# Feed-forward stages: the gated layer of one sequence merged into the attention of the next, in one block without barriers

## The reference

```
residual = hidden_states
x = _rmsnorm(hidden_states, ln1_w)
attn = _attention(x, Wq, Wk, Wv, Wo)
mod = MOD_SCALE * jnp.tanh(attn @ A)
h = _rmsnorm(residual, ln2_w)
gate_pre = h @ W_in_base.T + mod * (h @ A) @ B
gate = jax.nn.silu(gate_pre)
up = h @ W_up_base.T
mlp_out = gate * up @ W_down.T
return residual + mlp_out
```

## Time and profile before

| | before |
|---|---|
| median of 3 runs | 6643.49 us (6639.04 to 6646.93) |
| span of the profiled execution | 6647.8 us |
| PE, share of the span | 86% |
| DVE, ACT, POOL | 48%, 43%, 34% |
| mean granted PE clock | 0.90 of full |

### The profile page before, as it was taken

The page is one execution under the profiler, slowest core; times in us unless marked ns, Lnnn a source line. Parts: engine busy times, 40 slices in busy tenths (PEclk is TensorE's granted clock), DMA queues, the critical chain, the costliest instruction groups (busy, mean ns, idle before and its releaser), DMA issues. The chain is left out here.

```text
span 6647.8 us, 126185 instructions
## 1 busy us (share of the span) xinstructions
PE 5714.2 (86%) x53008; PEld 3756.8 (57%) x53008; DVE 3169.6 (48%) x4553; ACT 2831.9 (43%) x5153; POOL 2288.6 (34%) x1583
## 2 busy tenths in 40 slices
PE   6888798865889868888888888888899988889999
PEld 5776566543666436666665666666444446664444
DVE  5555433334333247666666766666411135564111
ACT  2323333444344345555555555555411146663111
POOL 4444000001000037666666666666422210002222
PEclk8988788877887889999999999999899998889999
DMA  0000000000000000000000000000111100002111
GB/s 27 2 2 33 0 0 0 14 0 31 0 0 0 2 23 21 17 16 23 16 16 23 16 16 16 23 16 16 75 42 40 42 27 0 0 0 93 42 40 46
DMA packets 60565, 136.36 MB, mean 21 GB/s; under 512 B 11638, under 2 KB 24054, under 8 KB 58842
## 3 DMA queue, kind: packets, MB, share of 16 engines
q1 hardware_dynamic: 60122, 129.79, 5.8%
HBM read 127.26 MB, written 2.50 MB: 20 GB/s over the span
## 5 line engine op out<-in xcount | busy, mean ns | idle before, releaser
L599 PE MATMUL ps<-moe_xn_all,moe_w 128*128 128x512 f32 x1792 | 808.3, 594 | 1.6 <-DVE moe_h L712 1.6
L712 DVE TENSOR_TENSOR moe_h<-moe_silu,ps 128x512 f32<-128x512 f32 x224 | 153.9, 687 | 935.8 <-ACT moe_silu L654 928.7
L599 PEld LDWEIGHTS ps<-moe_xn_all,moe_w 128*128 128x128 f32 x1792 | 340.3, 191 | 424.4 <-issue 421.6
L1539 DVE SCALAR_TENSOR_TENSOR kda_cv<-kda_pre,kda_w_front,kda_cv 128x1024 f32<-128x1024 f32 x297 | 561.1, 1907 | 1.4
L654 ACT ACTIVATE moe_silu<-ps 128x512 f32<-128x512 f32 x224 | 133.7, 597 | 986.1 <-PE ps L599 986.0
L1716 POOL TENSOR_TENSOR kda_g<-kda_g,kda_f 128x512 f32<-128x512 f32 x225 | 421.6, 1874 | 279.6 <-DVE kda_rows L1708 270.4
L555 POOL TENSOR_TENSOR moe_h<-moe_h,moe_cb 128x512 f32<-128x512 f32 x176 | 233.6, 1327 | 696.5 <-DVE moe_h L712 696.5
L609 PE MATMUL ps<-moe_h,moe_w 128*128 128x512 f32 x896 | 420.4, 592 | 0.0
L1427 PE MATMUL ps<-kda_xn_all,kda_w_front 128*128 128x512 f32 x808 | 374.4, 607 | 24.9 <-DMA kda_w_front<-in_Kw 22.5
L1708 POOL TENSOR_TENSOR kda_rows<-kda_q,kda_f 128x512 f32<-128x512 f32 x225 | 357.2, 1588 | 88.3 <-POOL kda_f L1717 52.8
L1798 PE MATMUL ps<-kda_x_sb,kda_t 64*64 64x32 f32 x5120 | 310.1, 221 | 0.0
(11 more groups left out here) (506 smaller groups left out, 12804.7 us busy)
## 6 DMA issues: line engine op xcount, KB each, us to landing
kda_col<-kda_beta SPq DMA_DIRECT2D x34, 512.0 KB, 4.1
moe_w<-in_Mw SPq DMA_DIRECT2D x6, 2816.0 KB, 19.6
moe_cb<-kda_beta SPq DMA_DIRECT2D x64, 256.0 KB, 3.1
kda_w_front<-in_Kw SPq DMA_DIRECT2D x34, 455.0 KB, 4.8
moe_cb<-kda_beta SPq DMA_DIRECT2D x32, 224.0 KB, 2.9
kda_w_out<-in_Kw SPq DMA_DIRECT2D x32, 192.5 KB, 4.7
moe_cb<-kda_beta SPq DMA_DIRECT2D x32, 192.0 KB, 2.8
moe_cb<-kda_beta SPq DMA_DIRECT2D x32, 160.0 KB, 2.7
```

The source lines that it names most:

```text
L599: last = nc.tensor.matmul(ps_gu[u % 2][r], w13[:, k, i, r], n.xn[:, k, cols(c)], start=k == 0, stop=k == KD - 1)
L1539: ins = nc.vector.scalar_tensor_tensor(cv[i % 2][:], pre[i % 2][:, :, j:j + SEQ], w_vec(w, K_CONV + i * CONV + j), cv[i % 2][:], ALU.mult, ...
```

## The change

The second block of `ffn` is written anew. The hardware loop is gone: one block holds all 8 sequences, written out, with running semaphore counts and no barrier until the end of the stage. There are 9 rounds. Round b works the attention of sequence b, group by group, and between its parts the gated layer of sequence b-1, unit by unit: group s goes with unit s. Round 0 has attention alone, round 8 the gated layer alone. At the end of a round stand the projections of the following sequence, spread among the last steps of the attention.

To fit into PSUM, scores have one pair of banks (1, 2) in place of two, and gate and up of a unit share the halves of one bank (3); only in round 8 does a second bank (1) alternate with it. So `scores(i)` waits until group i-1 is masked, and `up(u)` until `h` of unit u-1 is done. On ACT, `copy_out` of a group now stands ahead of the exponentials of the next. SiLU is made from tanh: ACT takes tanh(x/2), and DVE makes (tanh + 1) * x and then 0.5 * that * up, two instructions in place of one. Exponential and tanh share a table, which is loaded once per stage in the first block. The copy `x_seq` (DVE L1098) is left out; the values are projected from `n.xn` itself.

```diff
...
+EXP_TANH = "exp_and_others"
...
-        x_seq = s.sb("x_seq", [P, KD, SEQ])
...
+        ps_s = psum(g, 1, GH * SEQ).rearrange("p (j k) -> p j k", j=GH)
...
-        ps_g = [psum(g, 1 + i, SEQ) for i in range(2)]
-        ps_u = [psum(g, 3 + i, SEQ) for i in range(2)]
-        ps_y = [psum(g, 5, SEQ), psum(g, 0, SEQ)]
...
+        def ps_gate(u):
+            return psum(g, 1 if u >= (BATCH - 1) * FFN_T and u % 2 else 3, SEQ)
+
+        def ps_up(u):
+            return psum(g, 1 if u >= (BATCH - 1) * FFN_T and u % 2 else 3, 2 * SEQ)[:, SEQ:]
...
+                nc.scalar.preload_act_table_set(EXP_TANH)
...
-        with nc.Fori(0, BATCH) as b:
-            with nc.Block() as block:
...
+                def scores(i):
+                    b, q, t = i // GROUPS, i % GROUPS // FQ, i % FQ
+                    pe.wait_ge(m.q_in_sb, b + 1)
+                    pe.wait_ge(m.k_in_sb, b + 1)
+                    if i > 0:
+                        pe.wait_ge(m.masked_ready, i)
+                    w = keys(i) * P
+                    for j in (0, 2, 1, 3):
+                        tile, row = head_at(t, j)
+                        rows = slice(32 * row, 32 * row + 32)
+                        last = nc.tensor.matmul(ps_s[:, j, 0:w], qt[rows, tile, q * P:(q + 1) * P],
+                                                kt[rows, tile, 0:w], start=True, stop=True)
+                    last.then_inc(m.scores_ready, 1)
...
+                def up(u):
+                    b, f = u // FFN_T, u % FFN_T
+                    if u >= 1:
+                        pe.wait_ge(m.h_ready, u - 1 if u > (BATCH - 1) * FFN_T else u)
+                    own = slice(f * P, (f + 1) * P)
+                    for k in range(KD):
+                        nc.tensor.matmul(ps_up(u), w_up[:, k, own], n.xn[:, k, cols(b)], start=k == 0,
+                                         stop=k == KD - 1)
+                    for k in range(KD):
+                        nc.tensor.matmul(ps_gate(u), w_in[:, k, own], n.xn[:, k, cols(b)], start=k == 0, stop=False)
+                    pe.wait_ge(m.mod_in_sb, b + 1)
+                    nc.tensor.matmul(ps_gate(u), low_b[:, own], mod[:], start=False, stop=True).then_inc(m.gu_ready, 1)
+
+                def down(u):
+                    f = u % FFN_T
+                    pe.wait_ge(m.h_ready, u + 1)
+                    for k in range(KD):
+                        last = nc.tensor.matmul(ps_y[k], w_down[:, f, k * P:(k + 1) * P], h[:, u % 2],
+                                                start=f == 0, stop=f == FFN_T - 1)
+                    last.then_inc(m.down_done, 1)
...
+                queries(0)
+                key_rows(0)
+                values(0)
+                for b in range(BATCH + 1):
+                    here, before = b < BATCH, b > 0
+                    for s_ in range(GROUPS):
+                        i, u = b * GROUPS + s_, (b - 1) * FFN_T + s_
+                        if here:
+                            scores(i)
+                        if before:
+                            up(u)
+                        if here and s_ >= 1:
+                            turn(i - 1)
+                        if before and s_ >= 1:
+                            down(u - 1)
+                        if here and s_ >= 2:
+                            pv(i - 2)
+                    if before:
+                        down(b * FFN_T - 1)
+                    if here:
+                        end = (b + 1) * GROUPS
+                        pv(end - 2)
+                        if b + 1 < BATCH:
+                            queries(b + 1)
+                        turn(end - 1)
+                        low(b)
+                        pv(end - 1)
+                        turn_shares(b)
+                        if b + 1 < BATCH:
+                            key_rows(b + 1)
+                        modulate(b)
+                        if b + 1 < BATCH:
+                            values(b + 1)
...
+                def half_gate(u):
+                    act.wait_ge(m.gu_ready, u + 1)
+                    if u >= 2:
+                        act.wait_ge(m.half_ready, u - 1)
+                    nc.scalar.activation(gate[:, u % 2], ps_gate(u), ACT.Tanh, scale=0.5).then_inc(m.gate_ready, 1)
+
+                query_copy(0)
+                key_copy(0)
+                for b in range(BATCH + 1):
+                    here, before = b < BATCH, b > 0
+                    for s_ in range(GROUPS):
+                        i, u = b * GROUPS + s_, (b - 1) * FFN_T + s_
+                        if before:
+                            half_gate(u)
+                        if here and s_ >= 1:
+                            copy_out(i - 1)
+                        if here:
+                            exps(i)
+                    if here:
+                        if b + 1 < BATCH:
+                            query_copy(b + 1)
+                        copy_out((b + 1) * GROUPS - 1)
+                        shares_copy(b)
+                        if b + 1 < BATCH:
+                            key_copy(b + 1)
+                        modulate(b)
...
+                def gated(u):
+                    dve.wait_ge(m.gate_ready, u + 1)
+                    if u >= 2:
+                        dve.wait_ge(m.down_done, u - 1)
+                    nc.vector.scalar_tensor_tensor(h[:, u % 2], gate[:, u % 2], 1.0, ps_gate(u), ALU.add,
+                                                   ALU.mult).then_inc(m.half_ready, 1)
+                    dve.wait_ge(m.half_ready, u + 1)
+                    nc.vector.scalar_tensor_tensor(h[:, u % 2], h[:, u % 2], 0.5, ps_up(u), ALU.mult,
+                                                   ALU.mult).then_inc(m.h_ready, 1)
...
+                values(0)
+                for b in range(BATCH + 1):
+                    here, before = b < BATCH, b > 0
+                    for s_ in range(GROUPS):
+                        if here:
+                            maxima(b * GROUPS + s_)
+                        if before:
+                            gated((b - 1) * FFN_T + s_)
+                    if before:
+                        residual(b - 1)
+                    if here:
+                        widen(b)
+                        outputs(b)
+                        modulate(b)
+                        if b + 1 < BATCH:
+                            values(b + 1)
+                dve.wait_ge(m.x_done, KD * BATCH)
+        s.barrier()
...
```

More of the change, by code:

```diff
@@ L967, in ffn @@
         gate, h = s.sb("gate", [P, 2, SEQ]), s.sb("h", [P, 2, SEQ])
[L968 to L974 removed]
+        qt, kt = s.sb("qt", [P, FQ, SEQ]), s.sb("kt", [P, FQ, SEQ])
@@ L1044, in _ @@
                     for t in range(QT):
+                        at = b * SEQ + t * P
                         for k in range(KD):
-                            last = nc.tensor.matmul(ps_v[:, t], x_seq[:, k, t * P:(t + 1) * P], wv[:, k],
-                                                    start=k == 0, stop=k == KD - 1)
-                    last.then_inc(t_.v_ready, 1)
-                    attn_pe(nc, g, t_, pe)
+                            last = nc.tensor.matmul(ps_v[:, t], n.xn[:, k, at:at + P], wv[:, k], start=k == 0,
+                                                    stop=k == KD - 1)
@@ new lines, in turn, with pv @@
+                def turn(i):
+                    pe.wait_ge(m.probs_ready, i + 1)
+                    if i > 0:
+                        pe.wait_ge(m.pt_in_sb, i)
+                    for j in range(GH):
+                        for c in range(keys(i)):
+                            last = nc.tensor.transpose(ps_pt[:, j, c], p[:, i % 3, j, c * P:(c + 1) * P], g.ident[:])
+                    last.then_inc(m.pt_ready, 1)
+                def pv(i):
+                    b, q, t = i // GROUPS, i % GROUPS // FQ, i % FQ
+                    pe.wait_ge(m.v_in_sb, b + 1)
+                    pe.wait_ge(m.pt_in_sb, i + 1)
+                    for c in range(keys(i)):
+                        for j in range(GH):
+                            tile, row = head_at(t, j)
+                            last = nc.tensor.matmul(ps_ot[32 * j:32 * j + 32, t // per, q * P:(q + 1) * P],
+                                                    v[:, c, GH * tile + row], pt[:, i % 2, j, c],
+                                                    start=t % per == 0 and c == 0,
+                                                    stop=t % per == per - 1 and c == keys(i) - 1)
+                    last.then_inc(m.pv_ready, 1)
@@ L1050, in _, with turn_shares, low @@
+                def turn_shares(b):
+                    pe.wait_ge(m.shares_wide, KD * (b + 1))
+                    for q, k in product(range(QT), range(KD)):
+                        last = nc.tensor.transpose(ps_shares[:, k, q * P:(q + 1) * P], wide[:, q, k], g.ident[:])
+                    last.then_inc(m.shares_ready, 1)
+                def low(b):
+                    if b > 0:
+                        pe.wait_ge(m.x_done, KD * b)
```

(10 more changed lines are left out.)

199 lines of the change are left out of this document (133 added, 66 removed).

## The result

The changed kernel took 6381.07 us (median of 4 runs, 6371.59 to 6406.68) against 6641.34 for the kernel before beside it: a ratio of 0.961, 95% interval 0.9589 to 0.9631. The forecast was 6400.

A forecast was written before the change was run, and what follows sets the result against it. PE was taken to bound the kernel. Each feed-forward stage summed to 57 + 340.8 + 49.6 + 28.5 = 475.9 us, against 597.0 and 599.0 before; 6643.5 - 244 gave 6400 us, range 6345 to 6475.

The forecast's parts named there:

- The merged round: Rounds 1 to 6 of a feed-forward stage: PE's work 55.7 us plus 1.1 of waits, 56.8 us against 74.85 per sequence.
- the value between the bounds: A short group of attention at full clock, with no row to read: taken as 1.67 us, between 1.33 and 2.67.
- The end of the round: Queries, keys, values, four transposes and two low-rank products closing a merged round: 11.0 us of PE work.
- The waits: PE waits 0.8 us at unit 1 for `h` and some 0.3 at the last pv; other waits are met.
- rival 1: Clock falls in the merged rounds because every slot holds small tiles: 7026 us at half the clock; chance 0.05.
- rival 2: Wait on `h` binds in merged slots: delivered 2 us later, PE waits 1 us per unit, 6500 us; chance 0.14.
- rival 3: PE denser than priced, weight loads slipping under matmuls at half the gaps: 5.4 us a round less, 6324; chance 0.11.
- rival 4: Table loads were on the path before the change: 32 x 1.283 = 41 us more gain, 6359 us; chance 0.02.
- the 244: Saving summed over both feed-forward stages: 597.0 + 599.0 - 2 x 475.9 = 244 us less.
- The 6315: Time if all 32 table-set changes were on the path at the skill page's 2.66 us: a further 85 us, about 6315.
- Round 0: Attention without a partner, at the low clock, with first projections and 5 us for the earlier copy: together 57 us.
- The last rounds: Round 7, without projections, 49.6 us; round 8, gated layer as now plus the last addition, 28.5 us.

## Why the prediction was right

Step by step, as the prediction took them:

- **The merged round**, 56.8 forecast, 57.05 measured. A unit and a long group together: 3.41 + 2.67 = 6.08, measured 6.08. A unit and a short group: 5.08, measured 5.00, so the value between the bounds was near. The end of the round, 11.0 + 0.3, is 816.10 - 802.75 less turn and pv of the last group (1.18, 0.60): 11.6, and with that the whole excess of the round.
- **The waits.** Both that were named are the only two of PE in rounds 1 to 6. At unit 1 PE waited 1.36 us, where the forecast had priced 0.8 after the cover of a short scores. That reading was wrong, but it cost nothing:

```profile
759.69 1.13 PE L1154 MATMUL ps<-ffn_xn_all,ffn_w_up 128*128 128x256 f32 x4
...
761.62 0.48 PE L1159 MATMUL ps<-ffn_mod,ffn_low_b 16*128 16x256 f32 x1
761.62 0.49 PE L1104 MATMUL ps<-ffn_kt,ffn_qt 32*128 32x128 f32 x4
...
763.70 1.13 PE L1154 MATMUL ps<-ffn_xn_all,ffn_w_up 128*128 128x256 f32 x4 [1.36 <-DVE ffn_h L1325]
```

  The scores of group 1 run beside the unit's low-rank product, so they cover nothing and take no time of their own. From `up` of unit 0 to `up` of unit 1 it is 4.01 us, where 2.66 + 1.5 = 4.16 were forecast. The run with the values in slot 1 shows that the wait was worth its whole length.
- **The clock** (rival 1, the one that would have lost) stayed at 1.00 in rounds 1 to 7, against the earlier trace rows, where small tiles alone had 0.50. It was nearer than its 0.05 says: in the run with two further products, with a wait at unit 1 of 2.28 us in place of 1.36, some rounds had the low level.
- **The wait on `h`** (rival 2) does not bind: 1.07 us are left in a full short slot, where I had counted about 1, and 0.7 in the one ahead of unit 2. Six further products made it bind, and cost 222 us.
- **Denser PE** (rival 3): the gaps of 0.33, 0.20 and 0.17 us at changes of tile recur in every slot of the timeline of weight loads. Only the scores of group 1 are packed more densely, once a round (above).
- **Table loads** at nothing (rival 4): this was no rival to a sum of this form. The stage before was measured with its loads in it and the stage after was added up from PE's work, so whatever the loads cost lies in the 244 already, and 6359 counts it twice. What they cost the kernel before no run separates. In merged rounds the run with SiLU bounds them: 16 loads per round, 16 x 1.283 = 20.5 us, leave the round at 57.22. The Trainium skill, page "ScalarE: Activation LUTs", section "What ACT_TABLE_LOAD costs", puts a change of set at about 2.66 us with its drain. The trace has 1.283 for each load, and of 226 of them, less the saved product, the stages show about 5 us: beside PE's work a load took far less than either figure. The 6315 by that page's price counts twice as well.
- **Round 0**: 57 forecast, 57.98 measured, but the reason was wrong. The step that failed is "ACT now copies group i-1 before it starts the exponentials of group i ... I take 5". Undoing that order made round 0 2.6 us longer; giving it the second pair of score banks, with the order of before, made it 5.2 shorter. What the change took from round 0 is the look-ahead of the scores, not the order on ACT; that the total came out near was luck.
- **The last rounds**: 49.6 and 28.5 forecast, 1151.11 - 1101.37 = 49.7 and 1180.07 - 1151.11 = 29.0 measured (first scores of round 7, first `up` of round 8, end of the last addition). From the first weight load to that end the stage is 479.0 us, 475.9 forecast; but the next stage's centring now follows 3.2 us behind, 5.1 before, a gain that was not in the forecast: luck again. Centring to centring it is 656.4 - 536.0 = 120.4 less, 121.1 forecast; the second stage, with the recurrence ahead of it, 969.4 - 846.6 = 122.8 less, 123.1 forecast.

Against the median the forecast is 19 us high. Gqa's faster way, which the kernel before doesn't show in its profile, is 20.7 us, so nearly all of the difference lies in a stage whose code is unchanged.

## What to carry to other kernels

Where one engine is the bound in two phases, and in one of them it waits and runs at its low clock, working the other phase into it buys the clock as well as the waits; here PE's work fell by 10.6 us a round and its waiting by 3.8. Price such a merged loop from start to start of groups at the full clock, and count the slack of every wait that the shared banks bring. The slack deserves that care, since a wait that outgrows it can cost the wait and the clock behind it.

## What the runs showed of the hardware

**A short wait can cost the clock.** In the run with two further products a wait of 2.28 us was followed in round 3 by a stretch at 1.2 GHz, while the same wait in round 2, and the waits of 1.36 and 1.47 us in the merged rounds of the changed kernel's profile, were followed by none. In the run with two pairs in round 0 the wait of 1.47 us was. The lengths of the rounds recur in the same order (59.9, 58.2, 62.8), so it isn't chance from round to round; why the same wait does it once and not again was not settled.

**gqa runs in two ways.** The code of this stage is the same in all kernels, and one stretch of 500 us of it in the changed kernel's two profiled executions reads as follows, the slower first:

```profile
5250.00:5750.00 500.00, 422.25 (x3778) 309.25 (x3780) 303.14 (x507) 326.16 (x1024) 0.00 (x0) 0.86 0.00 0
```

```profile
5250.00:5750.00 500.00, 415.42 (x3986) 301.88 (x3984) 320.15 (x533) 343.27 (x1076) 0.00 (x0) 0.90 0.01 1
```

In the same time the second has 3986 matmul records against 3778, at a granted clock of 0.90 against 0.86; from gqa's first centring to that of the next stage it is 604.1 us against 626.1. The kernel before and the run with SiLU have the slower way (624.8 each), all other runs the faster one (604.0 to 604.2). What selects it stayed open. The changed kernel shows both ways; of the kernel before no execution beside these runs took less than 6633.97 us, where the faster way would bring its profiled span to 6647.8 - 20.7 = 6627.1. So it isn't shown that gqa is independent of the change: some 20 of the 260 us may be an effect of it on a stage that it doesn't touch. The first stage, rwkv, is unchanged too and takes 618.2 to 632.8 us in the twelve profiles. A difference of 20 us between two variants of this kernel means nothing until the changed stages have been read by themselves.
